# DLRM tower on one core: one transposed output store, constant compares for the first half's ids, layer one of tile 14 ahead of the last quad

## What is computed

```python
e = jnp.stack([tbl_0[ids[:, 0]], ..., tbl_26[ids[:, 26]]], axis=1)   # (2048, 27, 128)
dot = jnp.einsum('bnd,bmd->bnm', e, e)
z = dot.reshape(2048, 27 * 27)[:, idx]        # the 351 pairs i < j
h = jnp.concatenate([z, dense_ctx], axis=1)   # 367 wide
h = jnp.maximum(h @ W_top1 + b_top1, 0.0)     # 512
h = jnp.maximum(h @ W_top2 + b_top2, 0.0)     # 256
y = h @ W_top3                                # (2048, 1)
```

## Time and profile before

| | |
|---|---|
| time, median of 3 runs | 412.4 us (411.66 to 415.43) |
| the profiled execution | 412.63 us, span 410.5 us |
| PE busy / weight loads busy | 360.7 us (88%) / 323.2 us (79%) |
| DVE, ACT, POOL busy | 264.7, 166.6, 260.8 us |
| mean granted TensorE clock | 0.969 of full speed |
| chain that ended last | PE 75%, DMA 7%, issue 7%, ACT 4%, DVE 3%, SP's queue 2% |
| out_y stores | 16 transfers of 0.5 KB |
| PE's instructions | fetched by a DMA queue of their own: 48 packets, 0.79 MB |

### The profile page before, as it was taken

One profiled execution on the slowest core, in us unless ns is written; L12 is line 12 of the kernel. 1 busy time (PEld: TensorE's weight loads), 2 busy tenths in 40 slices (PEclk: granted clock), 3 DMA queues, 4 the chain that ended last, 5 costly groups with the idle time before them and its releaser, 6 DMA issues.

```text
span 410.5 us, 14146 instructions
## 1 busy us (share of the span) xinstructions
PE 360.7 (88%) x6136; PEld 323.2 (79%) x6136; DVE 264.7 (64%) x799; ACT 166.6 (41%) x229; POOL 260.8 (64%) x280
## 2 busy tenths in 40 slices
PE   1885899999999998999999988999799996989681
PEld 1665888989898888989898978988698986987571
DVE  4998798793869476865689375965549654642200
ACT  3666345543535344343535243244234433354020
POOL 6777777777777777777777777777777775000000
PEclk9999699999999999999999999999789998999997
DMA  7999853443333354334723383344523353000000
GB/s 189 239 251 239 207 122 91 95 91 79 87 84 83 94 65 93 79 93 80 94 71 96 77 56 105 78 93 79 85 71 85 87 69 51 3 2 3 3 0 0
DMA packets 25516, 36.65 MB, mean 89 GB/s; under 512 B 8464, under 2 KB 19728, under 8 KB 25456
## 3 DMA queue, kind: packets, MB, share of 16 engines
q0 software_dynamic: 8704, 17.84, 24.1%
q1 hardware_dynamic: 16752, 17.92, 18.1%
HBM read 35.73 MB, written 0.01 MB: 87 GB/s over the span
## 4 chain that ended last, share of the span: by engine, by line
PE 75%; DMA 7%; issue 7%; ACT 4%; DVE 3%; SPq 2%; ACTq 0%; DVEq 0%
PE embT_ps L320 37%; PE gram_ps L346 13%; PE h_ps L375 11%; PE h_ps L384 7%; DMA embT<-in_tbl 7%; PE embT_ps L330 6%; PE flat_ps L358 2%; ACT embT L499 2%; DVE one_hot L426 1%; ACT pairs L514 1%; DVE flat L455 1%; SPq L254 1%; DVE tbl L407 1%; ACT tbl L483 1%; SPq L247 0%
## 5 line engine op out<-in xcount | busy, mean ns | idle before, releaser
L297 POOL DMA_INDIRECT emb<-in_tbl,idx x272 | 259.9, 956 | 83.8 <-issue 81.1
L426 DVE TENSOR_SCALAR one_hot<-ids,row_of 125x256 fp32r<-125x256 int32 (+1 forms) x688 | 213.8, 384 | 55.5 <-PE embT_ps L320 52.0
L320 PE MATMUL embT_ps<-one_hot,tbl 125*128 125x256 f32 x1376 | 203.7, 300 | 20.7 <-DVE one_hot L426 19.6
L320 PEld LDWEIGHTS embT_ps<-one_hot,tbl 125*128 125x128 f32 x1376 | 182.0, 198 | 33.3 <-issue 14.3
L499 ACT COPY embT<-embT_ps 128x256 f32<-128x256 f32 x80 | 54.6, 682 | 159.3 <-PE embT_ps L320 159.3
L506 ACT COPY embT<-embT_ps 128x512 f32<-128x512 f32 (+1 forms) x80 | 87.9, 1101 | 1.5 <-PE embT_ps L330 1.4
L346 PE MATMUL gram_ps<-embT 128*27 128x27 f32 x4096 | 57.9, 193 | 15.3 <-issue 10.3
L346 PEld LDWEIGHTS gram_ps<-embT 128*27 128x27 f32 x4096 | 47.0, 105 | 30.9 <-issue 22.0
L375 PE MATMUL h_ps<-flatT,w_sb 126*128 126x256 f32 (+1 forms) x216 | 47.4, 374 | 0.0
L330 PE MATMUL embT_ps<-ident,emb 128*128 128x128 f32 x272 | 43.2, 275 | 0.0
L375 PEld LDWEIGHTS h_ps<-flatT,w_sb 126*128 126x128 f32 x216 | 38.0, 201 | 4.2
(11 more groups left out here) (19 smaller groups left out, 34.0 us busy)
## 6 DMA issues: line engine op xcount, KB each, us to landing
ids<-in_ids_hot SPq DMA_DIRECT2D x80, 128.0 KB
emb<-in_tbl,idx POOLq DMA_INDIRECT x272
embT<-in_tbl SPq DMA_DIRECT2D x7, 448.0 KB
embT<-in_tbl SPq DMA_DIRECT2D x3, 560.0 KB
w_sb<-in_W_ring SPq DMA_DIRECT2D x1, 756.0 KB
w_sb<-in_W_top SPq DMA_DIRECT2D x1, 512.0 KB
embT<-in_tbl SPq DMA_DIRECT2D x7, 52.0 KB
out_y<-y_sb SPq DMA_DIRECT2D x16, 0.5 KB
```

What stands on the lines that cost most here:

```text
L297: pool.indirect_dma_start(emb[:, t % EB, s, :], None, tables[f][:, :], bass.IndirectOffsetOnAxis(ap=idx[:, t, f:f + 1], axis=0),).then_inc ...
L320: mm = pe.matmul(out[:, 0:HN], tbl[0:ROWS, part, AT[o] + chunk, :], one_hot[0:ROWS, k % SLOTS, c, :], start=(chunk == 0 and part == 0), st ...
L426: done = dve.tensor_scalar(one_hot[0:ROWS, k % SLOTS, c, :], of, row_of[0:ROWS, KINDS.index(CH[o]), chunk:chunk + 1], None, ALU.is_equal)
```

## The change

Three edits.

1. The outputs are no longer stored tile by tile. When the last column of `y_sb` is there, PE turns the 128 x 16 block to 16 x 128 in `flat_ps`, DVE copies it to `h2`, and SP stores it in one transfer of 16 rows with 512 bytes each. SP's queue has only id loads between the weights and this store.
2. For the first half, ACT no longer only converts the ids to floats: it adds minus the first row number of the partition (`minus_row`, two small DVE instructions at the start) by an Identity activation with a bias of one value per partition. DVE then compares with the constant chunk number instead of with a column of `row_of`. That concerns 86 of the 688 compares.
3. Layer one of tile 14 runs ahead of the last quad (quad 4) of tile 15 instead of behind the products of tile 15. In `END` layer two of tile 14 moves to where it was.

```diff
         if t == T - 1:
-            after[3] += [("layer2", t - 3), ("ring", t - 1), ("flat", t - 1), ("layer2", t - 2)]
+            after[QUADS - 2] += [("layer2", t - 3), ("ring", t - 1), ("flat", t - 1), ("layer2", t - 2),
+                                 ("layer1", t - 1)]
...
-    END = [("dots", T - 1, 0, GROUPS32), ("layer1", T - 2), ("ring", T - 1), ("flat", T - 1), ("layer2", T - 2),
-           ("layer1", T - 1), ("layer2", T - 1)]
+    END = [("dots", T - 1, 0, GROUPS32), ("layer2", T - 2), ("ring", T - 1), ("flat", T - 1), ("layer1", T - 1),
+           ("layer2", T - 1)]
...
-        def store(sp, t):
-            sp.wait_ge(y_ready, t + 1)
-            sp.dma_start(y[t * TILE:(t + 1) * TILE, :], y_sb[:, t:t + 1]).then_inc(y_stored, 16)
...
-            stored = 0
             for n in range(O, len(HOTS)):
-
-                while HT * HOTS[n][1] - 1 >= stored + 7:
-                    store(sp, stored)
-                    stored += 1
                 load_ids(n)
-            for t in range(stored, T):
-                store(sp, t)
-            sp.wait_ge(y_stored, 16 * T)
+            sp.wait_ge(y_in_rows, 1)
+            sp.dma_start(y.rearrange("(t c) o -> t (c o)", c=TILE), h2[0:T, 0:TILE]).then_inc(y_stored, 16)
+            sp.wait_ge(y_stored, 16)
...
+            pe.wait_ge(y_ready, T)
+            pe.transpose(flat_ps[0:T, 0:TILE], y_sb[:, :], ident[:, :]).then_inc(y_turned, 1)
...
                 if n < O:
-                    dve.wait_ge(ids_as_floats, n + 1)
-                    of = of.bitcast(F32)
+                    dve.wait_ge(ids_relative, n + 1)
...
-                        done = dve.tensor_scalar(one_hot[0:ROWS, k % SLOTS, c, :], of,
-                                                 row_of[0:ROWS, KINDS.index(CH[o]), chunk:chunk + 1], None,
-                                                 ALU.is_equal)
+                        columns = one_hot[0:ROWS, k % SLOTS, c, :]
+                        if n < O:
+                            done = dve.tensor_scalar(columns, of.bitcast(F32), float(chunk), None, ALU.is_equal)
+                        else:
+                            done = dve.tensor_scalar(columns, of, row_of[0:ROWS, KINDS.index(CH[o]), chunk:chunk + 1],
+                                                     None, ALU.is_equal)
...
+            for i in range(len(KINDS)):
+                dve.tensor_scalar(minus_row[:, i:i + 1], row_of[:, i, 0:1], -1.0, None, ALU.mult).then_inc(rows_ready, 1)
...
+            dve.wait_ge(y_turned, 1)
+            dve.tensor_copy(h2[0:T, 0:TILE], flat_ps[0:T, 0:TILE]).then_inc(y_in_rows, 1)
...
-            def float_ids(n):
+            def relative_ids(n):
+
                 act.wait_ge(ids_loaded[n % IDS], 16 * (n // IDS + 1))
-                act.copy(ids[0:ROWS, n % IDS, :].bitcast(F32), ids[0:ROWS, n % IDS, :]).then_inc(ids_as_floats, 1)
+                if n == 0:
+                    act.wait_ge(rows_ready, 2 * len(KINDS))
+                kind = KINDS.index(CH[HOTS[n][2]])
+                act.activation(ids[0:ROWS, n % IDS, :].bitcast(F32), ids[0:ROWS, n % IDS, :], ACT.Identity,
+                               bias=minus_row[0:ROWS, kind:kind + 1]).then_inc(ids_relative, 1)
```

More of the change, by code:

```diff
@@ L159, in dlrm_tower @@
         row_of = sb("row_of", [P, len(KINDS), max(CH)])
+        minus_row = sb("minus_row", [P, len(KINDS)])
         embT = sb("embT", [P, TB, TILE, PITCH])
@@ L203, in dlrm_tower @@
         staged = [sem(f"staged{o}") for o in range(O)]
-        ids_as_floats = sem("ids_as_floats")
+        ids_relative = sem("ids_relative")
         high_ready = sem("high_ready")
@@ L225, in dlrm_tower @@
         y_ready = sem("y_ready")
+        y_turned = sem("y_turned")
+        y_in_rows = sem("y_in_rows")
         y_stored = sem("y_stored")
@@ L533, in _ @@
             split_high(0)
-            float_ids(0)
+            relative_ids(0)
             for kind, *of in ORDER:
@@ L537, in _ @@
                     split_high(ahead)
-                    float_ids(ahead)
+                    relative_ids(ahead)
                     ahead += 1
```

## The result

The changed kernel takes 389.54 us (median of 4 runs, 387.42 to 391.86), the kernel before 412.9 us (median of 4, 411.66 to 415.43). The ratio is 0.943 with a 95% interval of 0.934 to 0.951. The profiled execution took 391.86 us, its span is 390.1 us, against 412.63 and 410.5. Some executions of every kernel here are a few per cent slower than its others: the medians in this document are of all executions, the ratios and their intervals of the fast ones alone, so the two can differ by about one per cent.

What follows compares the result with a forecast made beforehand. The prediction took PE to be the bound, held up by 4-byte stores blocking its instruction fetches. Savings of 15.1 (body) + 4.2 (tail) + 3.5 (end) + 0.2 (start) = 23.0 us gave 389.5 us, range 385.5 to 397.5.

Steps and rivals of the forecast that it cites:

- The reading of the body: Layer-two stretches: 4-byte stores block DMA engines that PE's instruction fetches need; removing them saves 15.1 us, bounds 0 and 16.1.
- The 0.2 us per stretch: Five long layer-two stretches: amount held back from the 16.1 us excess for other variation, leaving 15.1.
- The tail: Last store: 7.0 us wait replaced by 2.0 plus 0.76 of transpose, copy and hand-overs; net 4.2 saved, bounds 4.4 and -0.8.
- The end: Layer one of tile 14 ahead of the last quad: layer one of tile 15 starts 3.5 us earlier, bounds 4.5 and 1.1.
- The standing is a fetch that was 2.0 us longer than the other, which leaves 1.4: Products of tile 15: PE's 3.43 us of standing shrinks to 1.0 us, bounds 0 and 3.43.
- a price of 1.7 us: End: if the clock falls again, layer one costs 4.57 instead of 2.84 us, making the bound -0.6.
- The start: Constant compares in the first half: 0.2 us saved, bounds -0.2 and 1.5, since the tables' landing sets the start.
- clock at full between 51 us and the tail: PE's granted clock over most of the span: full speed there was named as a sign the forecast is right.
- The long stretches that stay: Body: the place of PE's fetches, not stores, causes standing; 5.5 us saved in all, 407.1 us; chance 0.12.
- the half gain: Body: some standing returns elsewhere once the phase shifts, 7.5 us less gain, 397.1 us; chance 0.06.
- the slow single store: Tail: the one store also takes 7.0 us to be confirmed, whatever its shape, 394.6 us; chance 0.10.
- the slow case: ACT at the start: Identity needs another table, two loads of 1.28 us per activation, 415.3 us; chance 0.02.

Runs made afterwards that it cites:

- the stores alone: Kernel before with only its output stores replaced by one transposed store at the end: 389.38 us against 408.61, ratio 0.957.
- moved stores: Kernel before with its sixteen 4-byte-piece stores unchanged but all behind the last id load: 406.06 us against 408.61, ratio 0.999.
- the split kernel: Kernel before with one transposed store and layer one of tile 14 between two halves of tile 15's products: 386.17 us against the changed kernel's 388.23.
- the neighbouring scratch stores: Changed kernel plus seven extra body stores of 128 neighbouring 4-byte pieces into a scratch tensor: 421.43 us against 388.23.
- distant pieces: Changed kernel plus seven extra body stores into a scratch tensor, their 4-byte pieces 512 bytes apart: 390.60 us against 388.23.
- its run alone: Kernel before with only the first half's ids made relative and compared with constants: 410.75 us against 408.61, ratio 1.015.

## Why the prediction was right where it was

**The reading of the body was right.** The step from "stretches with stores are long, at a higher DMA share and equal GB/s" to "the 4-byte stores take the engines from PE's instructions" was an inference. Three runs carry it: the stores alone give the whole gain, moved stores move the loss, and seven stores put back bring it back unless their pieces lie apart. No stretch of the body without neighbouring stores has a piece of standing over 0.5 us. That the instruction fetch is the link between store and standing PE rests on less: the fetch of 3.0 us right behind a store in the earlier trace rows, against 0.9 in the changed kernel (0.23 x 0.25 x 16) even where PE stands:

```profile
373.75:374.00 0.25, 0.00 (x0) 0.00 (x0) 0.00 (x0) 0.00 (x0) 0.00 (x0) 1.00 0.23 66
```

The DMA records of the traces, read packet by packet, say more and leave the link argued. In the four kernels with stores to `out_y` three or four fetches behind stores took 2.7 to 3.5 us; in those with no neighbouring stores, none after 100 us took over 1.6. But the longest pieces of standing in the body are not explained by a long fetch: the one of 1.80 us at 289.90 ends just ahead of a fetch of 0.95 us (at 291.9), and with the neighbouring scratch stores, where PE stood 4.55 us in one piece from 255.15 us on, no fetch in the body took over 1.8. There the fetch came late: 16.8 us after the one before (244.6 to 261.4), where with distant pieces the same one, the 29th, came after 9.0. What did grow everywhere behind the stores is the 4 KB packets of the id loads: 2.0 us in the mean between 240 and 245 us before, 0.2 to 0.4 where no such store is near. Most of the higher DMA share is theirs.

The size was 17.0 us where I had 15.1. The 0.2 us per stretch that I held back had no ground; the stretches agree to 0.05 us, and the excess of 0.4 us in two layer-one stretches, which I took for natural spread, came from the stores as well: no kernel without neighbouring stores has a layer-one stretch over 22.82 us.

**The tail** brought 5.3 us, not 4.2. The landing was the mis-sized term: the wait was 1.0 us where I took 2.0, below even my lower bound, the load of 1.8 us. That bound was a time from issue to landing and not a wait; by the same measure the new store took 1.4. The transpose, the copy and the hand-overs were 0.69 us against 0.76. The 2.0 us of fixed cost that the prediction takes from the Trainium skill (page "DMA: Bandwidth & Descriptors", section "Anatomy of one DMA") are given there for transfers on GpSimd's path; SP issues this store, and its 1.4 us lie below them.

**The end** brought 1.9 us in the first profile and 0.9 in the second, not 3.5. The step that failed is "The standing is a fetch that was 2.0 us longer than the other, which leaves 1.4", of which I took 1.0. I subtracted the excess of one fetch's length from the standing as if PE had waited for just that fetch from its start. In the changed kernel the fetch has its normal length and PE stands 2.30 us, because the fetch begins only as PE stops (373.81 against 373.70 us) and PE goes on 1.3 us after it ends. Before, the fetch had begun at 383.8, 0.3 us ahead of the stop, and PE went on 0.8 us after its end. That 256 small matmuls in a row outrun the supply by themselves is my reading of the split kernel, in which the standing is gone. The clock then falls, which I had named with a price of 1.7 us and not taken. It cost less: 0.3 us in the last 91 small matmuls. Layer two of tile 14 takes 2.91 us in place of 1.99, but it lay under the work of DVE and ACT as forecast, and from the L454 of tile 15 to its layer one it is 3.7 us where I had 3.6. The 1.6 us missing are thus, to a tenth, 1.3 of standing, 0.3 of the slower matmuls and 0.2 behind them in layer one and its wait, less 0.3 by which the products began earlier than forecast.

**The start** was late by 3.8 us in the profiled execution where I had 0.2 us saved. The mechanism held: compares of 0.23 us instead of 0.32 (8 in 1.81 us) and nothing gained. The difference between the two profiles is chance for the larger part, since the same program in another execution had its first L454 at 61.39 us, earlier than the kernel before. A cost of the edit of some us, as its run alone had it, is not excluded. My sign "clock at full between 51 us and the tail" did not come: slice 7 (58 to 68 us) has 0.8.

**The rivals.** The long stretches that stay, the half gain and the slow single store did not happen: 21.0 us in all six, 17.0 us saved, a wait of 1.0 us. ACT shows a single load of its tables, so the slow case fell too:

```profile
L487 ACT ACT_TABLE_LOAD x1 | 1.3, 1283 | 0.7 <-PEq L582 0.7
```

The Trainium skill's statement that identity is in every set (page "ScalarE: Activation LUTs", section "Table sets: the hidden batching unit") agrees with that row.

## What to carry to other kernels

Many 4-byte pieces written next to each other in HBM were slow out of proportion here, lengthened other transfers and made PE stand: turn a column of results into rows and store it once, or look at the DMA share against the GB/s around such a store. When stretches of equal work grow along a kernel, line them up by a marker that comes once per tile before looking at any single wait. PE stood in a run of 256 tiny matmuls with no store about; work with longer instructions, which had to be done anyway, put in their middle removed the standing. Before a single execution's start is compared with another's, look how far two of the same program differ: here by 6.8 us.

## What the runs showed of the hardware

- A store of 128 neighbouring pieces of 4 bytes took 7.0 us of SP's wait alone and 9.8 us in the body; the same pieces 512 bytes apart had landed within 5 us in the body, and 16 pieces of 512 bytes in 1.4 us from issue to landing.
- PE stood for 2.1 to 2.5 us in a run of 256 small matmuls with no small store in flight, at the 166th or 191st, and not at all when 12 larger ones stood in the middle.
- Behind such stores the 4 KB packets of other loads took up to 2.0 us in the mean of 5 us, against 0.2 to 0.4 elsewhere.
- A compare of 256 columns with a constant took 0.23 us, with a value per partition 0.32 us (8 in 1.81 against 8 in 2.57 us). The activation with a bias per partition took 0.51 us where the plain conversion took 0.40.
- One chip ran the whole program 1.6 times slower, before and changed kernel alike, with 101 us in front of PE's small matmuls in which it waited for nothing that the profile shows. What made it so is not known from these runs.
